# Token shift of the FFN by transfers within SBUF, rank and step products in parts of the array, and another order of the first group's set-up

## The chip, the cores and the metric

The kernel runs on one core of one Trainium2 chip. The metric is the device time of one execution in microseconds (us). PE is TensorE, DVE VectorE, ACT ScalarE, POOL GpSimd and SP SyncE, which only issues transfers. A matrix product in fp32 appears in the trace as two records, each with a weight load.

## What is computed

16 sequences of 256 tokens with 128 features pass through a state-space layer and then through two layers of local attention and a gated feed-forward network. Cut to what matters here:

```
u = silu(causal_conv(x @ in_w))                     # 256 inner channels
delta = softplus((u @ dt1_w + dt1_b) @ dt2_w + dt2_b)     # through rank 16
h_t = exp(delta*A) * h_(t-1) + expansion*B*u              # 16 states per channel: scans
y = (sum_n C_n h_n + D*u) * silu(x @ gate_w);  x1 = layernorm(x + y @ out_w + out_b)
for each of two layers:
    q, k, v = shift_token(x1) @ wqkv;  l2norm, rotary, attention in windows of 64
    x2 = x1 + attention @ wo
    h = layernorm(shift_token(x2)) ;  x1 = x2 + (a * gelu(g)) @ w2 + b2,  a, g = h @ w1 + b1
shift_token(t): the second half of the features is taken from the token before (zero at the start)
```

The output is the layer norm of the last sum.

## The kernel before

**Groups and tiles.** The batch is cut into ten groups g of 1, 1, 2, 2, 2, 2, 2, 2, 1, 1 sequences (SIZES). A tile is 128 tokens, so a small group (one sequence) has two and a large one four. All attention work is done by tile q (64 of them over both layers), all feed-forward work by f, one of the 20 pairs of layer and group in QUAD; f = 0, 1, 3, 4, 15, 16, 18, 19 are small, the other twelve large.

**Order.** Every engine works through a list of named steps written out by hand: PE_ORDER, ACT_ORDER, DVE_ORDER, POOL_ORDER, SP_ORDER (lines 86 to 357). An engine issues strictly in that order; a step waits on semaphores for its inputs and for the buffer that it writes. State-space steps of later groups are interleaved with attention and feed-forward steps of earlier ones. Set-up code stands ahead of the lists.

**PSUM.** YY holds the state-space products, AA the query and key products and two parts of the FFN, BB scores and transposes, C values and attention outputs, M everything else: output projection (attn_out), shift, normalised transpose (norm_T), layer_T, up_a, down. `free` (line 1263) makes a step wait until the last user of its bank has been read.

**The state-space part.** u_in and gate_in (lines 1295, 1305) multiply with in_w and gate_w; convolve on DVE (line 1028); silu_u on ACT (line 834). rank (line 1312) forms the 16 rank values of all tokens of a group from both halves of the channels, ACT's rank (line 848) adds the bias, step_in (line 1321) multiplies with dt2_w, whose 17th row is the bias beside a row of ones in dt1_s. softplus (line 852) is Abs, Exp, Ln on ACT, step_size (line 1047) finishes delta on DVE. Then sixteen scans per group, each after its decay on ACT and followed by state_y on PE, which uses 64x64 parts of the array. Three buffers ring decays and scans.

**The feed-forward part of one f.** attn_out into M; attn_sum (line 1166) adds the residual into x2; shifted (line 1471) builds the shifted rows in M by three kinds of products per tile: identity for the first half of the features, a matrix `shift` for the second, and `carry` for the row that comes from the tile before; ffn_stats (line 1181) and ffn_norm (line 1193) on DVE read the shifted rows from M, ffn_rstd on POOL stands between them; then norm_T, up_gate, gelus, up_a, hidden, down, ffn_sum. residual (line 790) on POOL adds b2 to x2, once hn is written.

```
                    mm(M[:, lo:mid], ident[:, :], x2[:, i, 0:D // 2])
                    ins = mm(M[:, mid:hi], shift[:, :], x2[:, i, D // 2:], True, i % 2 == 0)
                    if i % 2:
                        ins = mm(M[:, mid:hi], carry[:, :], x2[:, i - 1, D // 2:], False, True)
```

**Transfers.** SP's list holds the loads of x and xT, the stores, and v_even: one or two copies per tile within SBUF of 64 rows of 2 KB (line 702). Before its list SP issues the first xT, gate_w, ident, out_w, four x and the large weights; ACT issues in_w, pv (columns of small weights), bv (rows of small weights, broadcast), the rank and step weights, mask and four rope tables (line 808).

**Set-up of the first group.** ACT issues its ten loads, does one activation for the table, then u_in 0 and the exponential of the rates (line 828). DVE zeroes buffers, convolves group 0, then coefficients (line 982), masks (line 1009) and rotation_tables (line 1015), then its list, which begins with step_size 0. POOL builds ident64, adds out_b to x, and builds diag (line 734), without which skip and state_y can't start.

## Time and profile before

| | us |
|---|---|
| median of three runs | 1104.92 |
| lowest and highest | 1102.85, 1107.98 |
| the profiled execution, its own time | 1106.03 |
| its span in the trace | 1103.8 |
| TensorE busy | 967.1 |
| VectorE busy | 863.2 |
| ScalarE busy | 832.3 |
| GpSimd busy | 671.5 |

Busy time of an engine is the time in which at least one of its instructions runs. Products are pipelined, so a record is longer (638 ns for 512 columns) than the distance to the next one; what a group of products occupies is read from the chain of waits, where pieces follow one another. The number after x is the count of records. The granted clock of TensorE is given as a share of its full 2.4 GHz.

### The profile page before, as it was taken

What the parts mean: (1) busy time and instruction counts of PE and PEld (TensorE: products, weight loads), DVE (VectorE), ACT (ScalarE), POOL (GpSimd) and SP (SyncE); (2) the same over time, 40 slices, a digit from 0 to 9 for tenths busy, and PEclk for the clock granted to TensorE, in tenths of its full rate; (3) what the DMA queues carried; (4) which work ended last, traced back from release to release, by engine and by line L of the source; (5) the groups of instructions that cost most, each with busy time, mean ns of one, the idle gap of its engine ahead of it and who ended that gap; (6) DMA issues with size and microseconds to landing.
All of it is one profiled execution on the core that took longest, in us unless ns stands there. A gap on an engine that the chain in (4) does not pass through costs nothing.

```text
span 1103.8 us, 27452 instructions
## 1 busy us (share of the span) xinstructions
PE 967.1 (88%) x10784; PEld 593.9 (54%) x10784; DVE 863.2 (78%) x1184; ACT 832.3 (75%) x1909; POOL 671.5 (61%) x513
## 2 busy tenths in 40 slices
PE   4677779799999899999999999998999999996775
PEld 1222345456555465557465646465665766665463
DVE  7776897898888877998799878996988875642543
ACT  4455777886998669886988699877879887783570
POOL 2004764688578666876567857685656777661561
PEclk9988899899999999999999999999999999998897
DMA  6000100000000100000000110010001011010010
GB/s 217 10 15 1 26 1 15 14 18 15 16 16 17 39 20 16 21 16 19 22 17 16 35 26 15 12 40 10 21 7 30 16 25 26 7 25 6 14 32 10
DMA packets 22354, 25.59 MB, mean 23 GB/s; under 512 B 2710, under 2 KB 14545, under 8 KB 22225
## 3 DMA queue, kind: packets, MB, share of 16 engines
q1 hardware_dynamic: 20783, 22.49, 7.9%
q8 instruction: 86, 1.41, 0.5%
q10 hardware_dynamic: 1442, 1.34, 0.4%
q14 instruction: 43, 0.35, 0.1%
HBM read 9.13 MB, written 2.10 MB: 10 GB/s over the span
## 4 chain that ended last, share of the span: by engine, by line
PE 47%; ACT 18%; issue 13%; DVE 11%; POOL 11%; ACTq 1%; POOLq 0%; DVEq 0%
PE M L1257 11%; PE YY L1257 10%; ACT prob L926 8%; PE AA L1257 8%; PE C L1257 6%; DVE scan L1073 4%; PE BB L1257 4%; POOL rn L761 4%; PE BB L1407 2%; PE BB L1395 2%; POOL rden L767 2%; PE C L1458 1%; ACT qkT L914 1%; ACT probT L895 1%; POOL kr L780 1%
## 5 line engine op out<-in xcount | busy, mean ns | idle before, releaser
L1073 DVE TENSOR_TENSOR_SCAN scan<-du,decay 128x1028 f32<-128x1028 f32 (+1 forms) x160 | 297.4, 1898 | 8.7 <-PE YY L1257 4.9
L926 ACT ACTIVATE prob<-BB,nbias,rn 128x128 f32<-128x128 f32 x472 | 208.7, 464 | 48.0 <-POOL nbias L774 47.3
L761 POOL TENSOR_TENSOR rn<-ssc,expo 128x16 f32<-128x16 f32 x64 | 212.5, 3321 | 19.8 <-ACT prob L926 15.1
L871 ACT ACTIVATE decay<-delta,negA 128x1024 f32<-128x1024 f32 (+1 forms) x160 | 153.3, 985 | 16.6 <-DVE scan L1073 12.1
L767 POOL TENSOR_TENSOR rden<-den,minus 128x8 f32<-128x8 f32 x64 | 126.5, 1976 | 49.5 <-ACT prob L926 49.5
L1257 PE MATMUL YY<-scan,diag 64*64 64x512 f32 (+1 forms) x1280 | 142.7, 538 | 15.3 <-DVE scan L1073 15.2
L1257 PE MATMUL AA<-wqkv,hT 128*128 128x512 f32 x256 | 131.4, 638 | 11.8 <-DVE qks L1148 10.2
L756 POOL TENSOR_SCALAR ssc<-ss 128x16 f32<-128x16 f32 x64 | 47.7, 745 | 91.1 <-DVE ss L1130 90.2
L1130 DVE TENSOR_REDUCE ss<-sq 128x16 f32<-128x1024 f32 x64 | 77.3, 1208 | 29.4 <-ACT sq L889 29.3
L926 ACT ACTIVATION_READ_ACCUMULATOR prob<-BB,nbias,rn 128x1 f32 x472 | 99.8, 211 | 0.0
L1162 DVE TENSOR_REDUCE nmax<-BB 128x8 f32<-128x1024 f32 x59 | 71.9, 1218 | 31.8 <-PE BB L1257 31.6
L889 ACT ACTIVATE sq<-AA 128x512 f32<-128x512 f32 x128 | 71.3, 605 | 22.7 <-PE AA L1257 22.5
L780 POOL TENSOR_TENSOR kr<-qkc,qks 128x512 f32<-128x512 f32 x64 | 84.7, 1323 | 5.9 <-DVE qks L1148 5.9
L914 ACT ACTIVATE qkT<-BB 128x512 f32<-128x512 f32 x118 | 64.2, 599 | 26.3 <-PE BB L1413 26.1
L1147 DVE TENSOR_TENSOR qkc<-AA,rope_c 128x1024 f32<-128x1024 f32 x64 | 77.7, 1214 | 5.2 <-PE AA L1257 2.4
L783 POOL TENSOR_TENSOR kr<-kr,rn 128x512 f32<-128x512 f32 x64 | 77.5, 1211 | 5.0
L1257 PEld LDWEIGHTS AA<-wqkv,hT 128*128 128x128 f32 x256 | 46.6, 199 | 62.7 <-issue 61.6
L1257 PE MATMUL M<-hnT,w 128*128 128x512 f32 (+3 forms) x160 | 71.9, 531 | 8.6 <-ACT hid L952 5.1
L1257 PEld LDWEIGHTS C<-v_even,probT 128*64 128x64 f32 x1024 | 64.5, 138 | 26.9 <-issue 18.7
L1148 DVE TENSOR_TENSOR qks<-AA,rope_s 128x1024 f32<-128x1024 f32 x64 | 77.6, 1213 | 0.0
L895 ACT ACTIVATE probT<-BB 128x1024 f32<-128x1024 f32 x59 | 60.8, 1030 | 22.2 <-PE BB L1395 20.9
L1257 PE MATMUL C<-v_even,probT 128*64 128x64 f32 x1024 | 73.1, 225 | 4.1 <-ACT v_odd L905 2.2
(158 smaller groups left out, 2062.4 us busy)
## 6 DMA issues: line engine op xcount, KB each, us to landing
v_even<-v_odd SPq DMA_DIRECT2D x96, 128.0 KB, 2.3
x<-in_x SPq DMA_DIRECT2D x6, 256.0 KB, 3.8
wqkv<-in_wqkv SPq DMA_DIRECT2D x1, 1536.0 KB
xT<-in_xT SPq DMA_DIRECT2D x6, 256.0 KB, 3.8
out<-outb SPq DMA_DIRECT2D x6, 256.0 KB, 2.6
w<-in_w SPq DMA_DIRECT2D x1, 682.0 KB
xT<-in_xT SPq DMA_DIRECT2D x4, 128.0 KB, 2.6
x<-in_x SPq DMA_DIRECT2D x4, 128.0 KB, 4.4
```

Source lines behind the costliest of these rows:

```text
L761: pool.tensor_tensor(rn[:, q % 2, :], ssc[:, :], expo[:, 0:2 * HEADS], ALU.pow).then_inc(rn_sb, 1)
L767: pool.tensor_tensor(rden[:, q % 2, :], den[:, q % 2, :], minus[:, :], ALU.pow).then_inc(rden_sb, 1)
L780: pool.tensor_tensor(kr[:, :], qkc[:, q % 2, 1, :], qks[:, q % 2, 1, :], ALU.add).then_inc(rope_add, 1)
L783: pool.tensor_tensor(heads(kr[:, :]), heads(kr[:, :]), rn[:, q % 2, HEADS:].unsqueeze(2).to_broadcast((P, HEADS, DH)), ALU.mult).then_inc( ...
L871: act.activation(decay[:, at % A_RING, both(g), 1:], delta[:, both(g), :], ACT.Exp, scale=negA[:, n:n + 1]).then_inc(decay_sb, 1)
L914: act.activation(qkT[:, :, :, lo:lo + WIN], bank_of(q, r)[:, :].rearrange("p (a c x) -> p a c x", a=2, c=PAIRS), ACT.Copy).then_inc(qkT_sb, 1)
L926: ins = act.activation(prob[:, h, :], bank_of(q, a)[:, c * P:(c + 1) * P], ACT.Exp, bias=nbias[:, q % 2, h:h + 1], scale=rn[:, q % 2, h:h ...
L1073: dve.tensor_tensor_scan(state, step, a, 0.0, ALU.add, ALU.mult).then_inc(scan_sb, 1)
L1130: dve.tensor_reduce(ss[:, :], sq[:, :, :].rearrange("p a (h x) -> p (a h) x", x=DH), AX.X, ALU.add).then_inc(ss_sb, 1)
L1147: dve.tensor_tensor(dst_c, src, cos, ALU.mult)
L1148: dve.tensor_tensor(dst_s, src[:, :, :, ::-1, :], sin, ALU.mult).then_inc(rope_mul, 2)
L1257: return pe.matmul(dst, lhsT, rhs, start=start, stop=stop, skip_group_check=True)
```

## The change

- **Shift.** The products of `shifted` are gone, and with them the matrices shift and carry. A step `shift` in SP's list waits for x2 and copies within SBUF into a new tile xs: 127 rows by one partition down (second half of the features), the carried rows, and the first half of the features unmoved. ffn_stats and ffn_norm read xs, after all three transfers; POOL's residual waits for them too. M is no longer held between attn_sum and norm_T.
- **Rank and step.** The tokens of a group are halved (k), and the rank product of each half of the tokens and of the channels (h) goes to its own 32 partitions of PSUM. dt2_w is laid out so that the step product adds both channel halves; it takes 64 rows of the array for each k. The bias step on ACT has half the columns, one Abs takes the place of two.
- **Set-up.** ACT issues two loads, SP the others, in a new order; tables are loaded explicitly; coefficients come ahead of the convolution; masks and tables become steps of DVE_ORDER; zeroing of qkT and v_even goes to POOL; silu_gate 0 comes ahead of silu_u 0.
- **Order.** All five lists are written anew. Shown are the stretches of PE around f = 17 (before and after), of DVE behind group 0, and the start of SP's.

```diff
 PE_ORDER = """
...
-up_a 16 1, up_a 16 2, out_T 58, layer_T 1 8, probs_T 59, down 16, weighted 59, out_T 59, attn_out 17, v_in 60,
-shift 17, norm_T 17, up_gate 17, v_in 61, qk_in 60, up_a 17 0, qk_in 61, layer_T 1 9, qk_T 60, up_a 17 1,
...
+down 16, weighted 59, out_T 59, attn_out 17, qk_in 61, v_in 60, qk_T 60, v_in 61, layer_T 1 9, scores 60,
+norm_T 17, up_gate 17, up_a 17 0, up_a 17 1, qk_in 62, qk_T 61, v_in 62, scores 61, probs_T 60, qk_in 63,
...
 DVE_ORDER = """
...
+scan 0 8, scan 0 9, scan 0 10, scan 0 11, scan 0 12, scan 0 13, scan 0 14, scan 0 15, gated 0, masks 0,
+mamba_sum 0, conv0 1, conv1 1, differences 1, mamba_norm 0, tables 0, step_size 1, scan 1 0, scan 1 1, scan 1 2,
...
 SP_ORDER = """
+load_xT 1, load_xT 2, v_even 0, v_even 1, shift 0, v_even 2, v_even 3, load_xT 3, v_even 4, v_even 5, shift 1,
+v_even 6, v_even 7, v_even 8, v_even 9, shift 2, load_xT 4, v_even 10, v_even 11, v_even 12, shift 3, shift 4,
+v_even 13, v_even 14, v_even 15, v_even 16, v_even 17, store 0, v_even 18, load_x 4, shift 5, load_xT 5,
+v_even 19, shift 6, v_even 20, v_even 21, v_even 22, v_even 23, v_even 24, v_even 25, store 1, load_x 5, shift 7,
...
-         "attn_out": "M", "shift": "M", "norm_T": "M", "layer_T": "M", "up_gate": "AM", "up_a": "M", "down": "M"}
+         "attn_out": "M", "norm_T": "M", "layer_T": "M", "up_gate": "AM", "up_a": "M", "down": "M"}
...
-        dt1_w = sb("dt1_w", [P, HALF, RANK])
-        dt2_w = sb("dt2_w", [RANK + 1, DI])
+        dt1_w = sb("dt1_w", [P, HALF, PART])
+        dt2_w = sb("dt2_w", [P, DI])
...
-        dt1_s = sb("dt1_s", [RANK + 1, TOK])
+        dt1_s = sb("dt1_s", [P, TOK // 2])
...
+        xs = sb("xs", [P, TILES, D])
...
+        def z_of(g):
+
+            n = tok_of(g) // 2
+            return YY[:, :].rearrange("p (k x) -> p k x", k=2)[:, :, 0:HALF * n].rearrange("p k (h x) -> p h k x", h=HALF)
+
+        def by_half(ap):
+
+            return ap.rearrange("p (h s) x -> p h (s x)", h=HALF).rearrange("p h (k x) -> p h k x", k=2)
...
+        A_W = 16 * 6
+        SHIFT = 16 * 3
...
             load_xT(0)
+            sp.dma_start(pv[:, :], t["pv"]).then_inc(w_cols, 16)
             sp.dma_start(gate_w[:, :], t["gate_w"]).then_inc(w_gate, 16)
+            sp.dma_start(dt1_w[:, :, :], t["dt1_w"].rearrange("(h p) r -> p h r", h=HALF)).then_inc(w_step, 16)
+            sp.dma_start(dt2_w[:, :], t["dt2_w"]).then_inc(w_step, 16)
             for dst, src in [(ident[:, :], t["ident"]), (out_w[:, :, :], t["out_w"].rearrange("(h p) n -> p h n", h=HALF))]:
                 sp.dma_start(dst, src).then_inc(w_mamba, 16)
+            sp.dma_start(bv[:, NST:], t["bv"][NST:].partition_broadcast(P)).then_inc(w_rows, 16)
             for g in range(X_RING):
                 load_x(g)
+            for dst, src in [(prob[:, 0:4, :], t["mask"]), (rope_c[:, 0], t["rope_c"]), (rope_s[:, 0], t["rope_s"]),
+                             (rope_c[:, 1], t["rope_c"]), (rope_s[:, 1], t["rope_s"])]:
+                sp.dma_start(dst, src).then_inc(w_rope, 16)
             for dst, src in [(wqkv[:, :, :], t["wqkv"].rearrange("l p n -> p l n")),
                              (wo[:, :, :, :], t["wo"].rearrange("l (c p) n -> p l c n", p=P)),
-                             (shift[:, :], t["shift"]), (carry[:, :], t["carry"]),
...
             def v_even_copy(q):
                 i = q % V_RING
+                if q == 0:
+                    sp.wait_ge(zeros_late, 1)
...
+            def shift(f):
+
+                n, mid = tiles_of(QUAD[f][1]), D // 2
+                sp.wait_ge(x2_sb, f + 1)
+                if f:
+                    sp.wait_ge(hn_sb, f)
+                else:
+                    sp.wait_ge(zeros_late, 1)
+                sp.dma_start(xs[1:P, 0:n, mid:], x2[0:P - 1, 0:n, mid:]).then_inc(sh_in, 16)
+                sp.dma_start(xs[0:1, 1:n:2, mid:], x2[P - 1:P, 0:n:2, mid:]).then_inc(sh_in, 16)
+                sp.dma_start(xs[:, 0:n, 0:mid], x2[:, 0:n, 0:mid]).then_inc(sh_in, 16)
+
+            run("SP", {"shift": shift, "load_xT": xT, "load_x": x, "store": store, "v_even": v_even_copy})
...
-                pool.wait_ge(w_rates, 16)
+                pool.wait_ge(w_rows, 16)
...
+            pool.memset(qkT[:, :, :, 0:WIN], 0.0)
+            pool.memset(xs[0:1, :, :], 0.0)
+            pool.memset(v_even[:, :, :], 0.0).then_inc(zeros_late, 1)
             pool.wait_ge(expo_ready, 2)
-            pool.wait_ge(zeros_ready, 1)
+            pool.wait_ge(zeros_late, 1)
...
             def residual(f):
                 l, g = QUAD[f]
-                pool.wait_ge(hn_sb, f + 1)
+                pool.wait_ge(sh_in, SHIFT * (f + 1))
...
-            for dst, src, sig in [(in_w[:, :], t["in_w"], w_first), (pv[:, :], t["pv"], w_first),
-                                  (bv[:, :], t["bv"].partition_broadcast(P), w_rates),
-                                  (dt1_w[:, :, :], t["dt1_w"].rearrange("(h p) r -> p h r", h=HALF), w_step), (dt2_w[:, :], t["dt2_w"], w_step),
-                                  (prob[:, 0:4, :], t["mask"], w_rope), (rope_c[:, 0], t["rope_c"], w_rope),
-                                  (rope_s[:, 0], t["rope_s"], w_rope), (rope_c[:, 1], t["rope_c"], w_rope),
-                                  (rope_s[:, 1], t["rope_s"], w_rope)]:
-                act.dma_start(dst, src).then_inc(sig, 16)
+            def load_table(n):
+                act.add_instruction(mybir.InstLoadActFuncSet(act_func_set_id=n, name=nc.get_next_instruction_name(),
+                                                             ins=[], outs=[]))
+
+            act.dma_start(in_w[:, :], t["in_w"]).then_inc(w_first, 16)
+            act.dma_start(bv[:, 0:NST], t["bv"][0:NST].partition_broadcast(P)).then_inc(w_rates, 16)
+            load_table(EXP_AND_LN)
+            act.wait_ge(w_rates, 16)
+            act.activation(negA[:, :], bv[:, BV["A_log"]:BV["A_log"] + NST], ACT.Exp).then_inc(a_exp, 1)
+            load_table(SILU)
             act.wait_ge(zeros_ready, 1)
-            act.activation(tack[:, :], zero[:, :], ACT.Exp)
-            act.wait_ge(w_first, F_W)
+            act.wait_ge(w_cols, 16)
...
             def rank(g):
-                act.wait_ge(d1_ps, g + 1)
-                act.activation(dt1_s[0:RANK, 0:tok_of(g)], Y[0][0:RANK, 0:tok_of(g)], ACT.Identity, bias=col("dt1_b", 0, RANK)).then_inc(d1_sb, 1)
+                n = tok_of(g) // 2
+                act.wait_ge(d1_ps, 2 * HALF * (g + 1))
+                act.activation(dt1_s[:, 0:n], Y[0][:, 0:n], ACT.Identity, bias=col("dt1_b")).then_inc(d1_sb, 1)
 
             def softplus(g):
                 load_table(EXP_AND_LN)
                 if g:
                     act.wait_ge(delta_sb, g)
-                for h in range(HALF):
-                    act.wait_ge(z_ps, HALF * g + h + 1)
-                    act.activation(th[:, ab(g, h), :], seqs(bk(Y[h], g)), ACT.Abs).then_inc(za_sb, 1)
-                act.wait_ge(za_sb, HALF * g + HALF)
+                act.wait_ge(z_ps, 2 * HALF * (g + 1))
+                act.activation(by_half(th[:, both(g), :]), z_of(g), ACT.Abs).then_inc(za_sb, 1)
+                act.wait_ge(za_sb, g + 1)
...
+            def state_weights():
+
+                dve.wait_ge(w_cols, 16)
...
-                for h in range(HALF):
-                    ins = dve.scalar_tensor_tensor(out=delta[:, ab(g, h), :], in0=seqs(bk(Y[h], g)), scalar=0.0,
-                                                   in1=th[:, ab(g, h), :], op0=ALU.max, op1=ALU.add)
+                for k in range(2):
+                    ins = dve.scalar_tensor_tensor(out=by_half(delta[:, both(g), :])[:, :, k], in0=z_of(g)[:, :, k], scalar=0.0,
+                                                   in1=by_half(th[:, both(g), :])[:, :, k], op0=ALU.max, op1=ALU.add)
...
-            rows = tiles(M[:, :])
-
             def ffn_stats(f):
                 l, g = QUAD[f]
-                dve.wait_ge(sh_ps, f + 1)
+                dve.wait_ge(sh_in, SHIFT * (f + 1))
                 for i in range(tiles_of(g)):
-                    ins = dve.bn_stats(f_st[:, i, :], rows[:, i, :])
+                    ins = dve.bn_stats(f_st[:, i, :], xs[:, i, :])
...
+            coefficients()
+            dve.wait_ge(w_cols, 16)
             convolve(0, 0)
             convolve(0, 1)
-            coefficients()
-            masks()
-            rotation_tables()
...
             def rank(g):
+
                 if g == 0:
                     pe.wait_ge(w_step, S_W)
                 pe.wait_ge(u_sb, g + 1)
                 pe.wait_ge(gate_sb, HALF * g + 1)
-                for h in range(HALF):
-                    ins = mm(Y[0][0:RANK, 0:tok_of(g)], dt1_w[:, h, :], u[:, ab(g, h), 1:], h == 0, h == HALF - 1)
-                ins.then_inc(d1_ps, 1)
+                n = tok_of(g) // 2
+                for k in range(2):
+                    for h in range(HALF):
+                        lo = (2 * k + h) * PART
+                        if SIZES[g] == 2:
+                            rhs = u[:, h * SIZES[g] + k, 1:]
+                        else:
+                            rhs = u[:, h, 1 + k * n:1 + (k + 1) * n]
+                        mm(Y[0][lo:lo + PART, 0:n], dt1_w[:, h, :], rhs).then_inc(d1_ps, 1)
 
             def step_in(g):
                 pe.wait_ge(d1_sb, g + 1)
                 pe.wait_ge(gate_sb, HALF * (g + 1))
+                n = tok_of(g) // 2
                 for h in range(HALF):
-                    mm(bk(Y[h], g), dt2_w[:, h * P:(h + 1) * P], bk(dt1_s, g)).then_inc(z_ps, 1)
+                    for k in range(2):
+                        mm(Y[k][:, h * n:(h + 1) * n], dt2_w[half(k), h * P:(h + 1) * P], dt1_s[half(k), 0:n]).then_inc(z_ps, 1)
...
-            def shifted(f):
-                l, g = QUAD[f]
-                pe.wait_ge(x2_sb, f + 1)
-                free("shift", f)
-                for i in range(tiles_of(g)):
-                    lo, mid, hi = i * D, i * D + D // 2, (i + 1) * D
-                    mm(M[:, lo:mid], ident[:, :], x2[:, i, 0:D // 2])
-                    ins = mm(M[:, mid:hi], shift[:, :], x2[:, i, D // 2:], True, i % 2 == 0)
-                    if i % 2:
-                        ins = mm(M[:, mid:hi], carry[:, :], x2[:, i - 1, D // 2:], False, True)
-                ins.then_inc(sh_ps, 1)
...
+    dt1_w = np.zeros((DI, PART), np.float32)
+    dt1_w[:, :RANK] = m["dt1_w"]
+    dt2_w = np.zeros((P, DI), np.float32)
+    for k in (0, P // 2):
+        dt1_b[k:k + RANK, 0] = m["dt1_b"]
+        dt1_b[k + RANK, 0] = 1.0
+        dt2_w[k:k + RANK] = m["dt2_w"]
+        dt2_w[k + RANK] = m["dt2_b"]
+        dt2_w[k + PART:k + PART + RANK] = m["dt2_w"]
```

## Rows read from the trace of the kernel before

**Rows 1.** The page, part 1: busy time, share of the span, instructions.
```profile
PE 967.1 (88%) x10784; PEld 593.9 (54%) x10784; DVE 863.2 (78%) x1184; ACT 832.3 (75%) x1909; POOL 671.5 (61%) x513
```

**Rows 2.** The windows of three stages; PEclk is the granted clock.
```profile
core 0: us, PE busy (x) PEld busy (x) DVE busy (x) ACT busy (x) POOL busy (x), PEclk, DMA share, GB/s
0.00:130.00 130.00, 81.01 (x588) 33.63 (x592) 98.88 (x145) 72.48 (x130) 34.06 (x32) 0.89 0.18 55
130.00:1000.00 870.00, 814.28 (x9491) 511.83 (x9492) 722.46 (x945) 716.52 (x1669) 596.75 (x440) 0.99 0.08 19
1000.00:1103.80 103.80, 71.83 (x711) 48.45 (x709) 41.83 (x95) 43.28 (x111) 40.69 (x42) 0.88 0.06 16
```

**Rows 3.** The page, part 4: the chain that ended last, by engine.
```profile
PE 47%; ACT 18%; issue 13%; DVE 11%; POOL 11%; ACTq 1%; POOLq 0%; DVEq 0%
```

**Rows 4.** Groups by form: count | busy, mean ns | idle before, releasers.
```profile
L1162 DVE TENSOR_REDUCE nmax<-BB 128x8 f32<-128x1024 f32 x59 | 71.9, 1218 | 31.8 <-PE BB L1257 31.6
...
L1185 DVE BATCH_NORM_STATS2 f_st<-M 128x6 f32<-128x128 f32 x64 | 14.6, 284 | 17.3 <-PE M L1257 17.3
```

**Rows 5.** Pieces of the chain of waits: start us, us, what.
```profile
264.23 1.91 PE AA L1257 x4
266.14 2.18 PE M L1257 x20
268.32 1.84 PE YY L1257 x16
...
1017.22 3.75 PE AA L1257 x4
```

**Rows 6.** The timeline of the first 32 us: start, us, engine, line, what [idle before].
```profile
7.04 1.28 ACT L816 ACT_TABLE_LOAD   x1 [7.04 <-issue]
...
8.44 0.82 ACT L824 ACTIVATE upre<-YY,pv 128x256 f32<-128x256 f32 x2
...
12.71 0.17 DVE L985 TENSOR_SCALAR tiny<-negA 128x16 f32<-128x16 f32 x1
12.83 0.63 ACT L839 ACTIVATE u<-hu 128x512 f32<-128x512 f32 x1 [2.16 <-DVE hu L1037]
12.90 0.72 POOL L721 TENSOR_TENSOR x<-x,bv 128x256 f32<-128x256 f32 x1 [5.01 <-DMA x<-in_x]
...
13.96 1.86 PE L1257 MATMUL YY<-u,dt_w 128*16 128x256 f32 x4 [2.88 <-ACT gate L846]
...
16.60 4.22 POOL L734 TENSOR_TENSOR diag<-ident,wsum 128x1088 f32<-128x1088 f32 x2 [2.98 <-DVEq L1007]
16.72 2.23 DVE L1013 CAST mask<-prob 128x512 bf16<-128x512 f32 x1
...
19.57 0.63 ACT L862 ACTIVATE th<-th 128x512 f32<-128x512 f32 x1
...
22.58 0.74 DVE L1052 SCALAR_TENSOR_TENSOR delta<-YY,th 128x256 f32<-128x256 f32 x2
...
24.24 7.95 DVE L1073 TENSOR_TENSOR_SCAN scan<-du,decay 128x514 f32<-128x514 f32 x7 [0.32 <-ACT decay L871]
```

**Rows 7.** The timeline at groups 1 and 2.
```profile
58.45 0.76 DVE L1052 SCALAR_TENSOR_TENSOR delta<-YY,th 128x256 f32<-128x256 f32 x2 [5.61 <-ACT th L862]
...
94.60 3.59 PE L1257 MATMUL YY<-u,dt_w 128*16 128x512 f32 x4 [4.87 <-ACT u L839]
```

**Rows 8.** Queue lines (packets, MB, share): v_even at 1009.3; store at 1074; last weights at 20.4.
```profile
q1 hardware_dynamic: 80, 0.13, 23.0%
v_even<-v_odd SPq DMA_DIRECT2D x1, 128.0 KB, 2.2
...
q1 hardware_dynamic: 504, 0.25, 14.3%
...
q1 hardware_dynamic: 62, 0.04, 34.9%
```

**Rows 9.** The timeline at f=17.
```profile
1015.18 1.08 PE L1488 MATMUL M<-ident,hn 128*128 128x128 f32 x4 [4.31 <-DVE hn L1199]
```

More of the change, by code:

```diff
@@ new lines @@
+sums 63, rope 63, hidden 17 2, attended 61, row_max 62, ffn_sum 17, final_stats 7, attn_sum 18, row_max 63,
+ffn_stats 18, final_out 7, ffn_norm 18, attended 62, attended 63, hidden 18 0, hidden 18 1, hidden 18 2,
+ffn_sum 18, attn_sum 19, final_stats 8, ffn_stats 19, ffn_norm 19, final_out 8, hidden 19 0, hidden 19 1,
+hidden 19 2, ffn_sum 19, final_stats 9, final_out 9"""
+POOL_ORDER = """
+bias 1, mamba_rstd 0, mamba_rstd 1, scale 0, rotate 0, scale 1, rotate 1, bias 2, exp_bias 0, bias 3, inverse 0,
@@ L360, in order @@
+v_even 38, load_xT 8, store 3, load_x 8, v_even 39, v_even 40, v_even 41, shift 11, v_even 42, v_even 43,
+v_even 44, shift 12, v_even 45, v_even 46, load_xT 9, v_even 47, v_even 48, store 4, v_even 49, load_x 9,
+shift 13, v_even 50, v_even 51, v_even 52, v_even 53, shift 14, v_even 54, v_even 55, store 5, shift 15,
+v_even 56, v_even 57, shift 16, v_even 58, v_even 59, shift 17, v_even 60, v_even 61, v_even 62, v_even 63,
+store 6, shift 18, store 7, shift 19, store 8, store 9"""
 def order(text):
@@ L422, in build @@
         identb = sb("identb", [P, P], BF16)
-        shift = sb("shift", [P, P])
-        carry = sb("carry", [P, P])
         mask = sb("mask", [P, 2, 2, P], BF16)
@@ L1232, in final_out @@
                 normalise(outb, outb, z_mv, z_rs, g, out_sb)
-            steps = {"conv0": lambda g: g and convolve(g, 0), "conv1": lambda g: g and convolve(g, 1), "differences": differences,
+            steps = {"masks": masks, "tables": rotation_tables, "conv0": lambda g: g and convolve(g, 0), "conv1": lambda g: g and convolve(g, 1), "differences": differences,
                      "step_size": step_size, "gated": gated,
@@ L1267, in free @@
                         pe.wait_ge(x2_sb, f + 1)
-                    elif last == "shift":
-                        pe.wait_ge(hn_sb, f + 1)
                     elif last == "norm_T":
@@ L1546, in _consts @@
     eye = np.eye(P, dtype=np.float32)
-    carry = np.zeros((P, P), np.float32)
-    carry[P - 1, 0] = 1.0
     return {"rope_c": tile(c), "rope_s": tile(s), "ident": eye,
-            "shift": np.eye(P, k=1, dtype=np.float32), "carry": carry,
             "mask": np.where(mask, 0.0, MASKED).astype(np.float32)}
```

533 lines of the change are left out of this document (255 added, 278 removed).

## The prediction, made before the changed kernel ran

> **What bounds the kernel now.** I read the page first: TensorE is busy for 967 of 1103.8 us, VectorE for 863, ScalarE for 832 [rows 1]. Then the windows, because a mean hides the stages. From 130 to 1000 us TensorE is busy 814 of 870 us (94%), VectorE 722 (83%), ScalarE 717 (82%); after 1000 us no engine reaches 70%, so there the length is that of a dependency chain [rows 2]. The chain of waits has TensorE for 47% of its length and ScalarE, VectorE and GpSimd for 40% together [rows 3]: in the middle TensorE sets the pace, but closely followed. The idle VectorE time is largely spent waiting for TensorE: 31.6 us before the row maxima, 17.3 us before the FFN statistics [rows 4]. The beginning is a chain too: ScalarE issues its ten loads until 7.04 us and only then loads a table and evacuates the first product, ready long before; VectorE converts masks and rotation tables from 16.72 to 22.58 us while delta, ready at 20.2, waits; the first scan starts at 24.24 [rows 6].
>
> **What the change takes from TensorE.** A token shift of a large group (two sequences, four tiles) is ten products, 20 records, 2.2 us at full clock [rows 5]; one of a small group is half of that, 1.1. There are 12 large and 8 small ones: 12 x 2.2 + 8 x 1.1 = 35 us. Of these 11 large and 6 small lie before 1000 us: 31 us.
>
> Rank and step products: four records of 128x512 take 1.91 us, so each of the two costs a large group about 1.8 us (two products) and a small one 0.9. The state products show what separate array parts give: sixteen records of 64-row, 64-column tiles with 512 columns take 1.84 us, 0.115 each, against 0.48 for a full one, four abreast [rows 5]. The new rank is four 128x32 products of half length abreast: 1.8 to 0.5 us if four run together, to 1.8 if none do. The new step is four products in two row halves: 1.8 to 0.95, or 1.8 if not abreast. No row has 32-column tiles; I take them abreast, as the nearest (64-column) tiles run. Saving 2.1 us per large group, 1.05 per small: from group 3 on 5 x 2.1 + 2 x 1.05 = 12.6 us. TensorE's relief in the middle is 31 + 12.6 = 43.6 us. It turns into time at somewhere between the 0.47 of the chain and the 0.94 of the window; I take 0.7, -31 us, if nothing new stalls.
>
> **Start.** ScalarE keeps two loads, does the rates' exponential and table before the product is evacuated, and evacuates at about 6.3 instead of 8.44. VectorE, however, now runs the coefficients (a dozen steps from 12.71 [rows 6], some 2.6 us) before the convolution: from 4.6 to 7.2, then 3.9 us of convolution to 11.1. Silu of u then starts at 11.1, not 12.83, and rank at 11.8, not 13.96 (gate is now activated first, hidden under the convolution). From rank to the end of the logarithm was 20.2 - 13.96 = 6.2 us; a shorter rank (-1.2) and bias step (-0.2) leave some 4.7: 16.5. Delta follows at once; the first scan starts at about 18.5, 5.7 us early. The price is the 5.9 us of masks and tables moved behind group 0. The tables go into a 5.61 us wait of VectorE for group 1's delta [rows 7], hidden; the masks stand ahead of the sum that frees group 1's first bank, where 1.3 us were idle: +1.2. The zeroing of v_even moves to GpSimd, which had nothing pressing before it adds out_b at 12.90 [rows 6]. The SP queue gets pv and the rank and step weights ahead of ident and out_w (+1.4 us) and the x loads (awaited to 12.90 before, say 15 now); adding out_b (0.72 us) and building diag (4.22 us) end near 20. Three scan buffers reach to 21.7 before a scan needs a state product: covered, with under 2 us to spare. Masks and ropes now ahead of wqkv add 0.77 MB, needed at 59 us: covered. Group 1 gains 1.8 us on its rank chain. Group 2's rank alone takes 3.59 us [rows 7], twice the 1.9 of four records at full clock (the granted clock is 0.89 on average up to 130 us [rows 2]): -2. Start: -5.7 + 1.2 - 1.8 - 2, taken as -8.
>
> **Small terms.** Normalising from SBUF instead of PSUM saves 0.04 us on 64 tiles; one absolute value for two and a bias step of half length save ScalarE some 3 us. Half of it shows: -2.
>
> **What the transfers cost.** A shift now is three DMAs on SP: 508 packets of 256 B over 127 rows, one or two packets of carry, 512 of 256 B; half for a small group. The trace has no such copy, so I bound it. A packet: v_even's 64 of 2 KB take 9.2 us of engine time (23.0% of 16 engines in a window of 2.5 us), 144 ns each, 18 ns for 256 B by bytes; a 512 B packet of a store takes 27 ns (14.3% of 16 engines in 6 us, 504 packets), so 18 to 27 ns. I take 18, since v_even also stays within SBUF. The fixed part of a landing is 2.2 us less four packets (0.6): 1.6 us [rows 8].
> How many of the 16 DMA engines carry it? If all, (508 + 512)/16 packets and two further issues of 0.45 us land the shift after 1.6 + 1.2 + 0.9 = 3.7 us. If the 127 rows run on one engine, after 1.6 + 508 x 18 ns = 10.8 us (15.3 at 27 ns), and 6.2 us (8.5) for a small group. The rows that bear on it: v_even's 64 rows are spread evenly, but the last load to land, with 85 rows, keeps only 35% of the engines busy [rows 8]. 127 is as little a multiple of 16, so I take one engine.
> The Trainium skill ("DMA: Bandwidth & Descriptors", section "Why a DMA increments its semaphore by 16 and not by 1") says the same more sharply: the engines are the largest number up to 16 that divides the outermost dimension, and 127 partitions give one. That rule speaks against this change; by it the landing is that of one engine, without it 3.7 us.
>
> Who waits: the FFN statistics, and behind them everything on VectorE. In the new order the steps between the residual sum and the statistics, each at the mean of its group of rows (a row maximum 1.22 us less some overlap [rows 4], a large scan 2.2), are 38.8 us for the 12 large shifts and 19.3 for the 8 small (for f=0 two scans; for f=17 nothing). In the middle the waits add 11 x 10.8 - 38.8 + 6 x 6.2 - 17.5 = 100 us. VectorE is idle for 148 us there already. If these waits take the place of idle time the stage is at least 722 + 100 = 822 us; if none do, 870 - 31 + 100 = 939. I take a third of the way, 861 (-9), since the idle time is mostly waits for TensorE, which runs ahead during a pause: it has 12 us of other steps between the output projection and the next transpose of a large f. v_even copies queue behind a shift on that engine, but are issued two tiles ahead of their use; SP otherwise waits most of the time.
>
> **End.** At f=17 statistics, normalisation and MLP stood alone: TensorE idle for 4.31 us [rows 9], then at half clock (3.75 us for four records instead of 1.91) [rows 5, 9]. Now tiles 60 and 61 are worked in between: -10. Against it: f=17 waits 10.8 instead of about 3.3 (+7.5), f=18 and f=19, with 1.2 us or less of work ahead, 6.2 instead of 1.5 (+3, +4.5): +5 in all.
>
> **Sum.** -8 - 9 + 5 - 2 = -14 on the profiled execution's 1106.0 us (span 1103.8 and 2.2 around it): 1092. The median of the runs, 1104.9, is 1.1 lower: 1091.
>
> **The rivals.** A change of 0.5%, 5.5 us, is about what a measurement tells from none.
> (A) All 16 engines carry the shift, landing in 3.7 us. For it: every 64- and 128-row copy in the trace; against: the 85-row load. Middle -31, end -10 + 3, start -8, small -2: -48, 1057. Chance 0.22.
> (B) Slower: one engine, and VectorE's queue passes the waits on. The place is the statistics step, in order ahead of the row maxima and rope that free TensorE's banks. It decides when the landing exceeds the 3 us of steps placed ahead of the statistics and the pause is not made up by idle time; with two thirds to nine tenths of the way from 822 to 939 the middle is 900 to 927, +30 to +57, in all +25 to +52: some 1135. For it: single M, C and A/B banks, all engines at 82 to 94%; against: the 148 us idle. Chance 0.25.
> (C) TensorE's relief is worth little because ScalarE and VectorE follow at once, and the waits eat the rest: middle +0, start -8, end +5, small -2: 1100. Chance 0.13.
> My forecast, one engine with most of the pause absorbed, has 0.40, and 1075 to 1110 as its own range.
> Also possible, inside these: the parts are not abreast (rank and step save nothing, +9), a shorter TensorE load lets its clock fall more often.
>
> **Range and chances.** 1056 leaves out half of A, 1134 half of B: 1056 to 1134. Faster by over 0.5% (under 1099.4): 0.30 of the forecast, 0.21 of A, 0.06 of C and 0.02 of B, 0.59; within 0.5%: 0.13; slower: 0.28.
>
> **What would show it.** The first scan at 18 to 19 us. No products from the shift matrices; TensorE busy some 50 us less. The rank's four products starting within a few ns, 0.5 us in all. The landing of xs, 10.8 us against 3.7: the most telling number. Waits of the statistics for DMA near 100 us, against 17. If xs lands in under 5 us the forecast is too slow, at any length of the middle; if it lands after 10 us and the span is over 1110, the absorption was wrong; if the middle is shorter than 850 with late landings, the order hides more than I count.

## The result, and the profile after

The changed kernel takes 1172.18 us in the median (1170.93 to 1173.75), beside 1104.45 for the kernel before: a ratio of 1.0609, 95% interval 1.0579 to 1.064. It is 68 us slower; 14 us faster was forecast, in a range that ended at 1134. The experiments below come to a version of the same three edits that is 2.2% faster than the kernel before.

The page, part 1 (busy us, share of the span, instructions), and part 4 (the chain that ended last, by engine), of the changed kernel:

```profile
span 1171.9 us, 27021 instructions
...
PE 948.7 (81%) x10544; PEld 571.8 (49%) x10544; DVE 856.7 (73%) x1180; ACT 832.8 (71%) x1898; POOL 666.6 (57%) x516
...
PE 42%; ACT 17%; DVE 13%; SPq 9%; issue 9%; POOL 5%; DMA 4%; ACTq 0%; POOLq 0%; DVEq 0%
```

TensorE's share falls from 88% [rows 1] to 81%, and two names are new in the chain [rows 3]: SyncE's issuing (SPq, 9%) and the transfers (4%). Together they are some 150 of 1172 us; followed step by step, the chain passes through the carry's issue at 18 of the 20 shifts.

The fixed windows of [rows 2] cut the two kernels at different steps. So I cut both where the residual sum x2 starts, at f=0 and at f=17. Windows of the changed kernel (stretch and length, then busy us of PE, PEld, DVE, ACT, POOL, granted clock, DMA share, GB/s):

```profile
130.30:1070.10 939.80, 805.16 (x9207) 493.30 (x9205) 718.02 (x948) 711.80 (x1656) 584.85 (x438) 0.93 0.09 22
1070.10:1171.90 101.80, 61.54 (x594) 39.61 (x593) 36.49 (x86) 41.34 (x107) 36.72 (x40) 0.79 0.09 22
```

And of the kernel before:

```profile
141.60:1007.60 866.00, 809.93 (x9427) 510.87 (x9420) 713.40 (x942) 710.22 (x1661) 585.23 (x436) 0.99 0.08 19
1007.60:1103.80 96.20, 65.72 (x638) 42.83 (x637) 40.81 (x93) 42.35 (x109) 40.69 (x42) 0.87 0.07 18
```

The start is 11.3 us shorter, the end 5.6 longer, and the middle 73.8 us longer: all of the loss is there. VectorE's idle time in the middle grows from 866.0 - 713.4 = 153 to 939.8 - 718.0 = 222 us. TensorE runs fewer products, yet is busy for only 5 us less, since its granted clock is 0.93 instead of 0.99.

The groups by form (count | busy, mean ns | idle before, releasers) of the changed kernel that answer to [rows 4]:

```profile
L1192 DVE TENSOR_REDUCE nmax<-BB 128x8 f32<-128x1024 f32 x59 | 71.9, 1218 | 38.5 <-PE BB L1285 38.5
L1227 DVE TENSOR_SCALAR hn<-xs,f_mv,f_rs 128x128 f32<-128x128 f32 x64 | 23.5, 426 | 3.6 <-POOL f_rs L777 3.4
L1213 DVE BATCH_NORM_STATS2 f_st<-xs 128x6 f32<-128x128 f32 x64 | 14.4, 282 | 97.9 <-DMA xs<-x 97.9
```

The statistics waited 17.3 us for TensorE's shift; now they wait 97.9 for the transfer. One shift in detail, f=6, from the timelines of SyncE (start us, us, what):

```profile
452.81 0.74 SPq L738 DMA_DIRECT2D xs<-x  x1
453.59 6.53 SPq L739 DMA_DIRECT2D xs<-x  x1
460.17 0.69 SPq L740 DMA_DIRECT2D xs<-x  x1
460.95 0.58 SPq L728 DMA_DIRECT2D v_even<-v_odd  x1
```

and of VectorE:

```profile
452.10 0.69 DVE L1207 TENSOR_TENSOR x<-M,x 128x512 f32<-128x512 f32 x1 [0.36 <-PE M L1285]
452.70 4.48 DVE L1103 TENSOR_TENSOR_SCAN scan<-du,decay 128x1028 f32<-128x1028 f32 x2
462.55 0.87 DVE L1213 BATCH_NORM_STATS2 f_st<-xs 128x6 f32<-128x128 f32 x4 [5.36 <-DMA xs<-x]
```

x2 ends at 452.79 and the statistics start at 462.55, 9.76 us later: two scans cover 4.4 of it, 5.36 are idle. SyncE issues the copy of 127 rows in 0.74 us, but then the next one, the one-row carry, holds it for 6.53 us; the third copy and v_even's come after that. What flows meanwhile, in the transfer view from 396.2 to 406 us (the shift of f=5; 40 slices of 0.245 us; the DMA row is the busy share of 16 engines in tenths):

```profile
DMA  0000000000000000000000000000000000059835
GB/s 0 0 0 0 0 2 15 16 15 16 14 15 18 17 18 18 19 18 19 18 18 19 18 18 19 18 18 19 18 18 19 18 20 18 18 130 230 192 126 150
```

For 7 us the share rounds to zero while a steady 14 to 20 GB/s moves; as soon as the third copy, of 128 rows, is on its way it is 126 to 230. 508 packets of 256 B at 18 GB/s are 7.2 us, one every 14 ns. From 397.6 to 404.8 the packets' own records add up to 0.08 of 16 engines' time, little more than one engine's. The trace doesn't name the engine of a packet, so that the 127 rows lie on a single one is a reading, which experiments 1 and 2 try.

The start in the timeline of the changed kernel, beside [rows 6]:

```profile
5.86 0.84 ACT L860 ACTIVATE upre<-YY,pv 128x256 f32<-128x256 f32 x2 [0.23 <-PE YY L1285]
...
10.99 0.63 ACT L868 ACTIVATE u<-hu 128x512 f32<-128x512 f32 x1 [1.95 <-DVE hu L1067]
...
11.72 0.66 PE L1285 MATMUL YY<-u,dt_w 128*32 128x128 f32 x8 [3.19 <-ACT u L868]
15.50 0.63 ACT L891 ACTIVATE th<-th 128x512 f32<-128x512 f32 x1
16.16 0.76 DVE L1082 SCALAR_TENSOR_TENSOR delta<-YY,th 128x256 f32<-128x256 f32 x2 [3.86 <-ACT th L891]
17.84 12.43 DVE L1103 TENSOR_TENSOR_SCAN scan<-du,decay 128x514 f32<-128x514 f32 x11 [0.20 <-ACT decay L900]
```

The first scan starts at 17.84 instead of 24.24.

### The profile page after: what moved, and what is told of

It reads as the page before. It is cut to its first block, busy times and chain, and to the rows that moved or that the text cites. A ratio compares the mean times of both kernels' runs of the same rounds, so it can differ in the third digit from the quotient of the medians.

```text
span 1171.9 us, 27021 instructions
## 1 busy us (share of the span) xinstructions
PE 948.7 (81%) x10544; PEld 571.8 (49%) x10544; DVE 856.7 (73%) x1180; ACT 832.8 (71%) x1898; POOL 666.6 (57%) x516
## 4 chain that ended last, share of the span: by engine, by line
PE 42%; ACT 17%; DVE 13%; SPq 9%; issue 9%; POOL 5%; DMA 4%; ACTq 0%; POOLq 0%; DVEq 0%
PE YY L1285 9%; PE M L1285 8%; SPq L739 8%; PE AA L1285 7%; ACT prob L955 6%; PE C L1285 6%; DVE scan L1103 4%; PE BB L1285 4%; DMA xs<-x 3%; PE BB L1442 2%; PE BB L1430 2%; PE C L1495 2%; POOL rn L795 1%; ACT hid L981 1%; ACT probT L924 1%
## 5 line engine op out<-in xcount | busy, mean ns | idle before, releaser
L1103 DVE TENSOR_TENSOR_SCAN scan<-du,decay 128x1028 f32<-128x1028 f32 (+1 forms) x160 | 292.8, 1871 | 13.4 <-ACT decay L900 7.8
L795 POOL TENSOR_TENSOR rn<-ssc,expo 128x16 f32<-128x16 f32 x64 | 215.6, 3369 | 13.7 <-ACT prob L955 8.9
L1285 PE MATMUL YY<-scan,diag 64*64 64x512 f32 (+1 forms) x1280 | 147.3, 552 | 24.9 <-DVE scan L1103 24.9
L1192 DVE TENSOR_REDUCE nmax<-BB 128x8 f32<-128x1024 f32 x59 | 71.9, 1218 | 38.5 <-PE BB L1285 38.5
L808 POOL TENSOR_TENSOR nbias<-nmax,rn 128x8 f32<-128x8 f32 x64 | 23.0, 360 | 126.6 <-DVE nmax L1192 126.0
L814 POOL TENSOR_TENSOR kr<-qkc,qks 128x512 f32<-128x512 f32 x64 | 90.6, 1416 | 6.1 <-DVE qks L1178 6.0
L1213 DVE BATCH_NORM_STATS2 f_st<-xs 128x6 f32<-128x128 f32 x64 | 14.4, 282 | 97.9 <-DMA xs<-x 97.9
L1285 PE MATMUL C<-v_even,probT 128*64 128x64 f32 x1024 | 75.3, 229 | 11.7 <-DMA v_even<-v_odd 5.4
L1285 PE MATMUL C<-wqkv,hT 128*128 128x512 f32 x128 | 74.6, 666 | 6.4 <-DVE o_s L1185 4.2
L1285 PE MATMUL M<-hnT,w 128*128 128x512 f32 (+3 forms) x160 | 75.0, 552 | 4.8 <-DVE hid L1236 3.3
```

The lines of the kernel that those rows point to most:

```text
L795: pool.tensor_tensor(rn[:, q % 2, :], ssc[:, :], expo[:, 0:2 * HEADS], ALU.pow).then_inc(rn_sb, 1)
L814: pool.tensor_tensor(kr[:, :], qkc[:, q % 2, 1, :], qks[:, q % 2, 1, :], ALU.add).then_inc(rope_add, 1)
L1103: dve.tensor_tensor_scan(state, step, a, 0.0, ALU.add, ALU.mult).then_inc(scan_sb, 1)
L1285: return pe.matmul(dst, lhsT, rhs, start=start, stop=stop, skip_group_check=True)
```

## The experiments

The kernel before was measured beside each set of experiments and took 1105.4 to 1107.2 us there in the median, so a ratio compares two experiments better than their times do.

My theory at this point (A): one DMA engine carries the 127 rows, and VectorE's in-order queue passes the wait on in full. Against it stood (B) the new order, or what queues on SyncE behind the copies, (C) the fall of TensorE's clock as a cause of its own, and (D) SyncE's 6.5 us at the carry rather than the transfer itself.

**1 and 2. The same rows in two copies.**

```
-sp.dma_start(xs[1:P, 0:n, mid:], x2[0:P - 1, 0:n, mid:])
+sp.dma_start(xs[1:113, 0:n, mid:], x2[0:112, 0:n, mid:])
+sp.dma_start(xs[113:128, 0:n, mid:], x2[112:127, 0:n, mid:])
```

> The changed kernel with its 127-row copy given as two, rows 1 to 112 and rows 113 to 127; same bytes, same order, one more issue on SyncE. Theory A (the 127-row copy lies on one DMA engine at 18 GB/s, its 9.7 us landing stalls VectorE's in-order queue 20 times, 97.9 us in all, and that is what costs): the copy of 112 rows spreads over 16 engines, the shifted tile is there about 4 us after x2 ends, the waits of f_st fall below 40 us, and the time to 1060 to 1085 us. Theory B (the loss is in the new order, or in the transfers that stand behind the copy on SyncE whatever its engines): waits of f_st may fall, the time stays above 1130. Theory C (the granted clock of 0.93 in the middle is the cause and not an effect): the clock stays 0.93 and the time above 1120.

Measured: 1096.05 us, ratio 0.9907 (0.9878 to 0.9936). One copy more, and 76 us less. The second kernel has, in place of the two added lines,

```
+sp.dma_start(xs[1:127, 0:n, mid:], x2[0:126, 0:n, mid:])
+sp.dma_start(xs[127:128, 0:n, mid:], x2[126:127, 0:n, mid:])
```

> The changed kernel with the copy given as 126 rows and 1 row. The divisor rule gives 126 = 14 x 9, so 14 engines: f_st starts about 4.5 us after x2's end and the time is within 10 us of the kernel with 112 + 15 rows. If instead only a multiple of 16 rows is spread, this kernel stands like the changed one: 9 to 10 us after x2's end, 1165 to 1175 us.

Measured: 1100.31 us, ratio 0.9932 (0.9907 to 0.9957). The groups of the statistics in the first and in the second kernel:

```profile
L1214 DVE BATCH_NORM_STATS2 f_st<-xs 128x6 f32<-128x128 f32 x64 | 14.3, 281 | 33.6 <-DMA xs<-x 33.6
```

```profile
L1214 DVE BATCH_NORM_STATS2 f_st<-xs 128x6 f32<-128x128 f32 x64 | 14.3, 281 | 32.8 <-DMA xs<-x 32.8
```

The wait falls from 97.9 to 33 us in both. So multiples of 16 are not what matters; 126 rows spread, 127 do not. The new order falls as main cause, since it is the same here, and so does C: the clock rises with the faster copy, from 0.917 to 0.951 over the span. The other part of B is not tried by this, since SyncE's long issue goes away together with the one-engine copy; experiment 12 prices two of the transfers that stood behind it. But the first came out 11 us above the range that I had given it, so a 5 us landing still costs something.

**3. The long copy issued last.**

```
-sp.dma_start(xs[1:P, 0:n, mid:], x2[0:P - 1, 0:n, mid:])
 sp.dma_start(xs[0:1, 1:n:2, mid:], x2[P - 1:P, 0:n:2, mid:])
 sp.dma_start(xs[:, 0:n, 0:mid], x2[:, 0:n, 0:mid])
+sp.dma_start(xs[1:P, 0:n, mid:], x2[0:P - 1, 0:n, mid:])
```

> The changed kernel with the 127-row copy issued last of the three, behind the one-row carry and the first half's copy; all else as it was. Theory A: the copy still takes its 7 us on one engine and starts some 1.4 us later, so f_st starts 8 to 10 us after x2's end and the time is 1155 to 1180 us, though the issue of the one-row carry no longer takes 6.4 us. Rival D (the 6.4 us in which SyncE is held at the carry's issue is what sets the landing, and the copy itself would be there sooner): f_st starts 4 to 6 us after x2's end and the time falls below 1130.

Measured: 1188.88 us, ratio 1.0739 (1.0697 to 1.0781), 8.9 above the upper end that I had given to A. SyncE's timeline at f=6:

```profile
456.37 0.66 SPq L738 DMA_DIRECT2D xs<-x  x1
457.07 0.66 SPq L739 DMA_DIRECT2D xs<-x  x1
457.77 0.72 SPq L740 DMA_DIRECT2D xs<-x  x1
458.59 6.39 SPq L728 DMA_DIRECT2D v_even<-v_odd  x1
```

D falls: the three shift copies are issued without a pause, and xs is there 10.7 us after x2, not 5. The pause moves to whichever transfer is issued behind the long one, now v_even's.

**4. Parts and set-up without the transfers.** The kernel before, with the rank and step products side by side and the new set-up; shift on TensorE, orders as before.

> The kernel before with two of the three parts of the change: rank and step products side by side in the array, and the first group's set-up in the new order (masks and rotation tables moved behind the first scans); the shift stays TensorE's product, the orders of the engines stay those of before. By the prediction's terms: set-up -8 (the trace of after has shown -11.4 at the first x2), parts up to -12.6 x 0.7 = -9 in the middle and 2 in the small groups: 1084 to 1094 us. If the middle takes up nothing of TensorE's relief (another engine bounds it): 1094 to 1098. If the early start does not last to the end: 1100 or more.

Measured: 1092.53 us, ratio 0.9875 (0.9831 to 0.992), within the first range. Two of the three edits bring 14 us, about what the forecast gave all three.

**5 and 6. VectorE's wait covered with other work.** Only VectorE's order changes; one of the 15 groups moved:

```
-... sums 26, scan 5 14, ffn_stats 7, scan 5 15, row_max 25, gated 5, ...
+... sums 26, scan 5 14, scan 5 15, row_max 25, gated 5, ffn_stats 7, ...
```

> The changed kernel, 127-row copy in one piece as it is; only VectorE's order differs: in groups 0 to 16 the statistics are moved back by 1 to 5 steps (scans, rotations, row maxima), as far as the other engines' orders allow, so that VectorE works while the copy lands; the landing itself stays 9.7 us. If the loss is VectorE's own waiting in its in-order queue: the waits of f_st fall from 97.9 to about 50 us and the time by about as much, to 1115 to 1130 us. If it is the longer way from x2 to the feed-forward's first product, which no order of VectorE shortens: the waits of f_st fall alike, the row maxima or the norm wait in their place, and the time stays 1160 to 1180.

Measured: 1196.14 us, ratio 1.0809 (1.079 to 1.0828). The waits of the statistics fall, as expected, but the time rises, above both of my ranges. VectorE's waits in this kernel (us in total, times, longest):

```profile
DVE nmax L1197 <- PE BB L1290: 80.1, 41, 10.0
...
DVE f_st L1218 <- DMA xs<-x: 31.8, 10, 9.7
```

and TensorE's:

```profile
PE M L1518 <- DVE hn L1232: 61.2, 10, 9.9
```

The statistics wait 66 us less, the row maxima 42 more (38.5 to 80.1), and TensorE waits 61.2 instead of 37.4 us for the normalized tile. What TensorE waited for in the middle alone, summed by the tile that ended the wait (us):

| TensorE waits for | before | 1 | the change | 5 |
|---|---|---|---|---|
| VectorE: attention output (o_s) | 4.4 | 6.6 | 22.0 | 5.3 |
| VectorE: scans | 4.7 | 4.1 | 13.3 | 4.7 |
| VectorE: normalized tile (hn) | 4.9 | 5.4 | 14.4 | 38.1 |
| ScalarE: attention weights (prob) | 14.4 | 14.7 | 13.0 | 35.3 |
| transfers | 0 | 5.9 | 17.7 | 17.9 |
| everything | 54.2 | 84.2 | 132.3 | 152.9 |

Beside kernel 1 the changed kernel waits longer above all for steps that stand behind the statistics in VectorE's order: 15 us more for attention outputs and 9 for scans, beside 9 for the normalized tile and 12 for transfers. So VectorE's in-order queue does pass its pause on, as theory A has it. The move in this experiment takes those waits away, but gives back more: the statistics now stand behind steps that end after xs has landed (they start 176.6 us behind x2, summed over the 17 shifts of the middle, instead of 142.8), and TensorE, which has the feed-forward's first transpose in its own fixed order, stops there, with the scores behind it. So this cover costs more than it saves; VectorE's pause by itself is not priced by it.

> The kernel with the copy as 112 + 15 rows (1096 us, waits of f_st 33.6 us), VectorE's statistics moved back by 1 to 3 steps in groups 0 to 16. If VectorE's waiting is what costs: waits of f_st about 12 us, time 1070 to 1080. If the way from x2 on costs: 1094 to 1100, or longer by what the moved steps add.

Measured: 1123.67 us, ratio 1.0172 (1.0141 to 1.0203), the same once more: waits of the statistics 16.5 instead of 33.6 us, and 28 us slower, with the statistics 122.7 instead of 86.2 us behind x2.

**7. The order of before, with fast transfers.**

> The kernel before with all three parts of the change, the copy as 112 + 15 rows, but the engines' orders of the kernel before (TensorE's shift steps taken out, the copies put into SyncE's order where x2 ended before). It tells how much of the 1096 us is the new order. If the orders of the change are worth something with fast transfers: 1100 to 1115. If they were laid out for another landing than the chip's and cost: 1080 to 1092.

Measured: 1148.66 us, ratio 1.039 (1.0347 to 1.0434), above all that I had expected. With the same copies the order of the change is worth 53 us, though SyncE's order here is mine and may be part of it. One cost in it is seen (below, under what I had not expected).

**8 and 11. Set-up alone, parts alone.**

> The kernel before with the new set-up order alone. With both parts it was 1092.5, 14.7 below the kernel before. By the term of the prediction this one gives -8: 1097 to 1100, and the parts the other 6 to 7. If the set-up gives all of the early start on: about 1095.

Measured: 1098.74 us, ratio 0.9936 (0.9917 to 0.9955).

> The kernel before with the rank and step products side by side in the array alone. Both parts together gave -14.7 (-1.25%), the set-up alone -6.6 (-0.64%): if they add up, this one gives -6 to -8, 1097 to 1100 (the prediction's terms: 12.6 x 0.7 = 9 and 2). If the set-up's early start is what lets the parts' relief through: 1103 to 1105.

Measured: 1100.28 us, ratio 0.9953 (0.9938 to 0.9968). This is 0.3 us above what I had expected. The two give 0.64% and 0.47%, together 1.1%, beside 1.25% (0.8 to 1.7) for both: they add up within the interval.

**9. The unshifted half by VectorE.** 112 + 15 rows, and instead of the fourth transfer

```
-sp.dma_start(xs[:, 0:n, 0:mid], x2[:, 0:n, 0:mid])
+dve.tensor_copy(xs[:, 0:tiles_of(g), 0:D // 2], x2[:, 0:tiles_of(g), 0:D // 2])
```

> The kernel with the copy as 112 + 15 rows (1096 us, f_st 5.0 us behind x2's end in the mean, 20 times), and the unshifted half of the columns copied by VectorE itself instead of by a fourth transfer: one issue less on SyncE (0.7 to 0.9 us), one VectorE copy of about 0.3 us more. Each microsecond on the way from x2 has cost about its own length so far (9.7 to 4.9: 71 us of way, 76 us of time). So f_st 4.1 to 4.3 us behind x2, way -0.8 x 20 = -16, time 1080 to 1088, below both kernels of the case. If the way no longer bounds it at this length and the time is set by the row maxima and TensorE: 1094 to 1100.

Measured: 1081.33 us, ratio 0.9775 (0.9749 to 0.9801), as expected, and faster than both kernels of the case.

**10. The normalization earlier.**

> The same, and in 8 of the 20 groups (0, 1, 3, 5, 7, 10, 12, 13) VectorE's normalization moved 1 to 5 steps forward, as soon as GpSimd can have the reciprocal root; the counterpart of moving the statistics back, which cost 24 and 27 us. If any lengthening of the way costs because TensorE waits behind it, a shortening gains where TensorE has waited: few groups here, 0 to -8 against the kernel without it. If the order laid out is the balanced one and every step moved past loses its place: 5 to 20 us slower than without.

Measured: 1086.66 us, ratio 0.9827 (0.9804 to 0.985), 5 us slower than without. The normalized tile is ready 24 us sooner behind x2, summed over the shifts of the middle, but then lies 32 us longer until TensorE takes it, which is 7 us later behind x2 than without the move: what was moved past lost more than was won.

**12. Two loads ahead of the shifts.**

```
-... shift 2, load_xT 4, ... shift 5, load_xT 5,
+... load_xT 4, shift 2, ... load_xT 5, shift 5,
```

> The changed kernel, one copy of 127 rows as it is; in SyncE's order the loads of groups 4 and 5 stand ahead of the shifts 2 and 5 and no longer behind them. In the changed kernel TensorE waits for these two loads 6.0 and 6.3 us, 12.3 in all (2.3 with 16 engines), since the issue of the carry holds SyncE for 6.4 us. If the loss of 68 us is in part these late loads: both waits gone and about 10 us less, 1160 to 1164. If the slow way from x2 covers them anyway: 1168 to 1173.

Measured: 1167.72 us, ratio 1.0558 (1.0532 to 1.0583). TensorE's waits for a transfer from 130 us on, in the changed kernel:

```profile
PE YY L1285 <- DMA xT<-in_xT: 12.3, 2, 6.3
PE C L1285 <- DMA v_even<-v_odd: 5.4, 1, 5.4
```

Both waits for the loads are gone, 12.3 us, and the time falls by 4.5: a third of it shows, between my two cases. The gain is small beside the noise; the intervals of the two ratios still touch.

**All of them by the distance.** From the timelines I summed, over the 17 shifts of the middle, the time from x2's end to the first statistics record. "Middle" is from x2's start at f=0 to that at f=17; the clock is that of the span.

| kernel | x2 to statistics, us | middle, us | clock | time, us |
|---|---|---|---|---|
| before (shift on TensorE) | 66.1 | 866.0 | 0.967 | 1104 to 1107 |
| 4, parts and set-up | 66.9 | 862.6 | 0.968 | 1092.5 |
| 9, half by VectorE | 74.5 | 858.9 | 0.960 | 1081.3 |
| 1, 112 + 15 rows | 86.2 | 870.5 | 0.951 | 1096.1 |
| 7, order of before | 87.3 | 903.4 | 0.936 | 1148.7 |
| 6, 112 + 15 rows, statistics moved back | 122.7 | 895.7 | 0.943 | 1123.7 |
| the change | 142.8 | 939.9 | 0.917 | 1172.2 |
| 3, long copy last | 158.7 | 953.7 | 0.913 | 1188.9 |
| 5, statistics moved back | 176.6 | 963.0 | 0.904 | 1196.1 |

From kernel 9 to 1, to the change and to 3 the middle grows with the distance, 11.6 us for 11.7, 69.4 for 56.6 and 13.8 for 15.9: up to the change nothing is absorbed. In 5 and 6, beside the kernels that they were made from, it grows by 23.1 for 33.8 and 25.2 for 36.5. The distance isn't all: kernel 7 has that of kernel 1, and its middle is 33 us longer.

Part of each microsecond is the clock's. The middle of kernel 9:

```profile
127.50:986.30 858.80, 779.41 (x9207) 478.94 (x9205) 723.12 (x965) 710.41 (x1656) 586.09 (x438) 0.98 0.09 22
```

It has the same 9207 products as the change, at 0.98 instead of 0.93, and is busy for 779.4 instead of 805.2 us with them. The clock is lower where TensorE is idle for longer: 56 us of the middle at 0.99 (before), 79 at 0.98 (9), 87 at 0.97 (1) and 135 at 0.93 (the change). So 26 of the 81 us between the two middles are slower products, and 55 are waiting. I have no run that holds the clock, so that split is read from the trace, not shown by an experiment.

## Why the prediction was wrong

**Start, predicted -8: right in kind, and larger.** The first scan starts at 17.84 (18.5 predicted) and x2 of f=0 11.3 us earlier. The set-up alone gives 0.64%, 7 us.

**Rank and step, predicted 12.6 us of TensorE in the middle: right.** The groups by form of the changed kernel:

```profile
L1285 PE MATMUL YY<-dt_s,dt_w 64*128 64x256 f32 x48 | 6.8, 402 | 0.7 <-ACT dt_s L880 0.7
L1285 PE MATMUL YY<-dt_s,dt_w 64*128 64x128 f32 x32 | 4.4, 418 | 3.5 <-ACT dt_s L880 3.5
L1285 PE MATMUL YY<-u,dt_w 128*32 128x256 f32 x48 | 4.3, 432 | 5.5 <-ACT u L868 5.5
L1285 PE MATMUL YY<-u,dt_w 128*32 128x128 f32 x32 | 2.2, 351 | 8.3 <-ACT u L868 8.3
```

and of the kernel before, with the shift's:

```profile
L1257 PE MATMUL M<-x,ident 128*128 128x64 f32 x128 | 24.9, 276 | 0.9 <-DVE x L1177 0.6 <-ACT hT L881 0.3
L1257 PE MATMUL M<-x,shift 128*128 128x64 f32 x128 | 24.7, 275 | 0.0
L1257 PE MATMUL YY<-u,dt_w 128*16 128x512 f32 x24 | 13.1, 671 | 4.9 <-ACT u L839 4.9
L1257 PE MATMUL M<-x,carry 128*128 128x64 f32 x64 | 12.4, 275 | 0.0
L1257 PE MATMUL YY<-dt_s,dt_w 17*128 17x512 f32 x24 | 11.9, 613 | 0.0
L1257 PE MATMUL YY<-dt_s,dt_w 17*128 17x256 f32 x16 | 6.4, 534 | 1.1 <-ACT dt_s L850 1.1
L1257 PE MATMUL YY<-u,dt_w 128*16 128x256 f32 x16 | 5.8, 503 | 7.1 <-ACT u L839 4.3 <-ACT gate L846 2.9
```

37.2 us of rank and step products become 17.7: the parts do run abreast (48 records of 432 ns within 4.3 us). In the middle of kernel 11, which has the parts alone, TensorE is busy for 798.9 instead of 809.9 us. The shift's three groups (identity, shift, carry) interleave and are pipelined, so their times can't be added; together their records cover 39 us, 35 predicted.

**One engine, predicted landing 10.8 and 6.2 us: right.** The statistics start 9.7 and 5.9 us behind x2; a packet follows the last after 14 ns, not 18. The rule of the Trainium skill's "DMA: Bandwidth & Descriptors" (section "Why a DMA increments its semaphore by 16 and not by 1"), by which 127 rows lie on one engine, agrees with the runs: 127 rows move at 18 GB/s, and with 112 + 15 or 126 + 1 rows the statistics start about 5 us behind x2.

**Waits of the statistics, predicted 100 us more in the middle: too high.** They are 79.3 there, 65 more than the 13.9 of the kernel before.

**The middle, "a third of the way" from 822 to 939: the step that failed.** The prediction took two thirds of the pause as absorbed and came to 861 us; the middle measured 939.9, and nothing was absorbed. Its argument was that VectorE's idle time is mostly waits for TensorE, "which runs ahead during a pause". Neither came. Apart from the waits of the statistics, VectorE is idle for 139 us of the middle before and for 142 after, so the new waits took the place of no old ones. And TensorE did not run ahead: its own idle time in the middle grew from 56 to 135 us, most of the growth in waits for VectorE's steps behind the pause, for the normalized tile and for transfers (the table at experiment 5). Experiment 1 shows by one edit that the landing is what does it: 56.6 us less from x2 to the statistics, 69.4 us less of middle. Experiments 5 and 6 show that moving VectorE's steps does not buy it back, since every engine's order is fixed around that way.

My rival B had the sign and the place (VectorE's in-order queue), but kept a tenth to a third as absorbed; TensorE's own order, which stops at the transpose, passes the delay on too. That the measured 939.9 meets the upper end of 939 is partly luck. That end was 870 - 31 + 100; with the 5 us less of TensorE's busy time and the 65 more of waits that were measured, the same sum gives 866 - 5 + 65 = 926. The late loads of experiment 12 are part of the other 14 us; the rest stays open.

**TensorE's relief, predicted -31 in the middle: not there.** Of 43.6 us of fewer products 5 were left: the granted clock fell from 0.99 to 0.93, which the prediction named in half a sentence and priced at nothing. In kernel 9, at 0.98, 809.9 - 779.4 = 30.5 us are left.

**The queue, priced at nothing ("SP otherwise waits most of the time"): wrong.** SyncE is held for 6.4 us at the issue behind each large shift; two loads came 6 us late, worth 4.5 us (experiment 12), and TensorE waited 5.4 us once for a v_even copy (not tried by itself; 3.6 in kernel 1).

**The end, predicted +5: right.** 101.8 instead of 96.2 us, +5.6: a sum of the order's gain and three uncovered landings. From x2 to the statistics these three take 15 us more than before, as predicted, which leaves some -10 for the order; no run has the two apart.

With 112 + 15 rows the transfers and the new order are worth nothing against the shift on TensorE (1096.1 and 1092.5); with three issues instead of four, another 15 us less, they are worth 11.

## What to carry to other kernels

Count the rows of a transfer before its bytes: a copy of 127 rows took 7 us here at 18 GB/s, where one of 128 rows moved at 126 to 230, and giving it as 112 and 15 rows took 76 us off the kernel. Where all engines follow fixed orders and are busy for 80 to 95% of a stage, don't count on their idle time as a reserve: here a longer way between two dependent steps came out as added time in full (69 us for 57), its loss of clock included. And look at what stands behind a long transfer on the issuing queue, not only at who reads it.
